# The last quarter of the columns of the masked product in pruning moved to GpSimd, its row sums to ScalarE

## The reference

```python
edge_scores = softmax(cos * H, axis=1)              # cos = xn @ xn.T
edge_mask = (edge_scores >= th_edge) & comp_mask[:, None]
H_pruned = H * edge_mask                            # the masked product
connectivity = H_pruned.sum(axis=1)                 # its row sums
node_scores = softmax(connectivity * feat_mag)
node_mask = (node_scores >= th_node) & (connectivity > 0)
vdeg = maximum(H_pruned.sum(axis=1), EPS)
edeg = maximum(H_pruned.sum(axis=0), EPS)           # its column sums
agg = (H_pruned.T * dv_isqrt) @ transformed * de_inv[:, None]
msg = dv_isqrt[:, None] * (H_pruned @ agg)
```

## Time and profile before

| what | us |
|---|---|
| median of 3 runs | 2627.26 (2624.27 to 2629.78) |
| the profiled execution | 2625.25 |
| its span, first to last instruction | 2623.5 |
| VectorE busy | 1647.2 (63%) |
| TensorE busy | 2146.1 (82%) |
| ScalarE busy | 768.6 (29%) |
| GpSimd busy | 4.1 |
| pruning's row blocks, first iteration | about 708 to 1068 |
| pruning's row blocks, second iteration | about 1691 to 2051 |

### The profile page before, as it was taken

One profiled execution on the slowest core, in us unless ns is written; L12 is line 12 of the kernel. 1 busy time (PEld: TensorE's weight loads), 2 busy tenths in 40 slices (PEclk: granted clock), 3 DMA queues, 4 the chain that ended last, 5 costly groups with the idle time before them and its releaser, 6 DMA issues. The chain is left out here.

```text
span 2623.5 us, 36440 instructions
## 1 busy us (share of the span) xinstructions
PE 2146.1 (82%) x15204; PEld 748.1 (29%) x15224; DVE 1647.2 (63%) x1785; ACT 768.6 (29%) x856; POOL 4.1 (0%) x16
## 2 busy tenths in 40 slices
PE   6769879799776566799999799776666799969998
PEld 2224243232221111244453233221111244432222
DVE  7870043288698888755523288698888755555553
ACT  0010010166443333111110166443333111125554
POOL 0000000000000000000000000000000000000000
PEclk9999989999887887899999999887887899979999
DMA  9958989799389898977779799389898977747770
GB/s 387 424 251 360 408 345 424 321 378 373 145 352 375 357 363 354 375 258 258 274 312 427 323 380 378 152 358 378 356 362 353 369 258 258 285 197 257 262 272 28
DMA packets 119369, 836.03 MB, mean 319 GB/s; under 512 B 8512, under 2 KB 10560, under 8 KB 76608
## 3 DMA queue, kind: packets, MB, share of 16 engines
q1 hardware_dynamic: 117184, 832.63, 80.4%
q10 hardware_dynamic: 2048, 1.35, 0.2%
HBM read 698.68 MB, written 135.27 MB: 318 GB/s over the span
## 5 line engine op out<-in xcount | busy, mean ns | idle before, releaser
L786 DVE CUSTOM_DVE_ANT_0 stream<-ps,stream 128x1024 f32<-128x1024 f32 x504 | 594.3, 1221 | 134.8 <-DMA stream<-in_adj 92.6
L797 ACT ACTIVATE stream<-stream,negmax 128x4096 f32<-128x4096 f32 x128 | 474.9, 3710 | 594.9 <-DVE negmax L791 594.9
L753 PE MATMUL ps<-edgeT,node_twice 64*128 64x512 f32 x1024 | 294.4, 699 | 253.1 <-DVE mx L786 253.1
L401 PE MATMUL ps<-stream,stage 128*64 128x512 f32 x1792 | 401.8, 599 | 62.1 <-DMA stream<-in_adjT 36.5
L1118 DVE SCALAR_TENSOR_TENSOR stream<-stream,cut 128x4096 f32<-128x4096 f32 x62 | 278.0, 4484 | 6.3
L753 PE MATMUL ps<-edgeT,query_twice 64*128 64x512 f32 x1024 | 245.4, 612 | 6.4 <-DVE edgeT L817 3.9
L1078 PE MATMUL ps<-stream,xw 32*64 32x512 f32 x4096 | 229.5, 589 | 0.6 <-ACT xw L1161 0.6
L753 PEld LDWEIGHTS ps<-edgeT,node_twice 64*128 64x128 f32 x1024 | 98.7, 210 | 440.6 <-DVE mx L786 330.4
L401 PEld LDWEIGHTS ps<-stream,stage 128*64 128x64 f32 x1792 | 127.0, 138 | 330.2 <-issue 285.1
L768 PE MATMUL ps<-stream,ones 128*1 128x512 f32 x1024 | 181.0, 844 | 8.2 <-DVE stream L1118 8.2
L1343 ACT ACTIVATE stream<-ps,bits_bias 128x1024 int32<-128x1024 f32 x128 | 142.4, 1114 | 108.1 <-PE ps L1308 107.2
(11 more groups left out here) (180 smaller groups left out, 1461.7 us busy)
## 6 DMA issues: line engine op xcount, KB each, us to landing
stream<-in_adj SPq DMA_DIRECT2D x178, 2048.0 KB, 11.8
stream<-in_adjT SPq DMA_DIRECT2D x74, 2048.0 KB, 12.2
pruned<-stream SPq DMA_DIRECT2D x64, 2048.0 KB, 7.7
spare<-pruned SPq DMA_DIRECT2D x22, 2048.0 KB, 11.2
query_twice<-pruned SPq DMA_DIRECT2D x22, 2048.0 KB, 11.4
node_twice<-pruned SPq DMA_DIRECT2D x20, 2048.0 KB, 11.5
query_twice<-in_adjT SPq DMA_DIRECT2D x7, 2048.0 KB, 35.3
node_twice<-in_adjT SPq DMA_DIRECT2D x7, 2048.0 KB, 35.2
```

The costliest lines, as they stand in the source:

```text
L401: last = nc.tensor.matmul(ps[F * h:F * h + F, bank + b, :], stage[:, t.k % SL, :], half_bank(src, b, h), start=False, stop=False, skip_gro ...
L753: last = nc.tensor.matmul(ps[:, 2 * slot + h, :], stationary[F * h:F * h + F, rows_n], bank_of(edgeT[F * h:F * h + F, :], c), start=True, ...
L786: nc.vector.tensor_tensor_reduce(out=prod[s][:, cols], in0=ps[:, 2 * slot:2 * slot + 2, :].rearrange("p a b -> p (a b)"), in1=block_in[:, ...
L797: nc.scalar.activation(prod[s], prod[s], ACT.Exp, bias=negmax[:, s:s + 1], accum_out=zsum[:, s:s + 1]).then_inc(exp_done, 1)
```

## The change

`prune(t)` on VectorE now does columns 0 to 3071 (`LEFT = 3 * CHUNK`) with the same instruction. GpSimd waits for `cut_ready` and does columns 3072 to 4095 in two instructions, a comparison with the cut in place, and, after a wait for its own first one, a product with the block in place. ScalarE copies these 1024 columns into an unused buffer for the sake of their row sums, one block later than its exponentials. SyncE's store and TensorE's column sums wait for both parts. VectorE waits for ScalarE's sums, before it takes the slot again and at the end, and adds the two row sums.

```diff
+                conn_right, conn_ready = st["mean"], sem("row_sums_added")
+                kept_right, right_summed = sem("right_columns_kept"), sem("right_columns_summed")
+                pruned, pruned_right = sem("left_columns_pruned"), sem("right_columns_pruned")
+                LEFT = 3 * CHUNK
+                unused = moved[:, 0:16, :].rearrange("p n f -> p (n f)")
...
                     def store(t):
                         s = t.k % SL3
                         sp.wait_ge(pruned, t.n + 1)
+                        sp.wait_ge(pruned_right, t.n + 1)
...
                         pe.wait_ge(pruned, t.n + 1)
+                        pe.wait_ge(pruned_right, t.n + 1)
...
                         nc.vector.scalar_tensor_tensor(
-                            out=prod[s], in0=prod[s], scalar=cut[:, s:s + 1], in1=buffer(t),
-                            op0=ALU.is_ge, op1=ALU.mult,
+                            out=prod[s][:, 0:LEFT], in0=prod[s][:, 0:LEFT], scalar=cut[:, s:s + 1],
+                            in1=buffer(t)[:, 0:LEFT], op0=ALU.is_ge, op1=ALU.mult,
                             accum_out=st["conn"][:, bass.ds(t.block, 1)]).then_inc(pruned, 1)
...
                         wait(dve, summed, t.n - 2)
+                        wait(dve, right_summed, t.n - 2)
...
                     dve.wait_ge(pruned, NB)
+                    dve.wait_ge(right_summed, NB)
+                    v = nc.vector
+                    v.tensor_tensor(st["conn"][:, :], st["conn"][:, :], conn_right[:, :], ALU.add)\
+                        .then_inc(conn_ready, 1)
+                    dve.wait_ge(conn_ready, 1)
+
+                @block.gpsimd
+                def _(pool):
+                    def body(t):
+                        s = t.k % SL3
+                        right = prod[s][:, LEFT:N]
+                        pool.wait_ge(cut_ready, t.n + 1)
+                        nc.gpsimd.tensor_scalar(right, right, cut[:, s:s + 1], None, ALU.is_ge).then_inc(kept_right, 1)
+                        pool.wait_ge(kept_right, t.n + 1)
+                        nc.gpsimd.tensor_tensor(right, right, buffer(t)[:, LEFT:N], ALU.mult)\
+                            .then_inc(pruned_right, 1)
+                    for n in range(NB):
+                        body(last_step(n, seq))
...
+                    def sum_right(t):
+                        act.wait_ge(pruned_right, t.n + 1)
+                        wait(act, right_summed, t.n)
+                        nc.scalar.activation(unused, prod[t.k % SL3][:, LEFT:N], ACT.Copy,
+                                             accum_out=conn_right[:, bass.ds(t.block, 1)]).then_inc(right_summed, 1)
+
+                    def body(t):
+                        exponentials(act, t, max_ready, exp_done)
+                        if t.k >= 1:
+                            sum_right(t.back(1))
+                    row_blocks(act, 3, LEAD, body, seq)
+                    sum_right(last_step(NB - 1, seq))
```

More of the change, by code:

```diff
@@ L927, in build @@
                 seen = sem("scores_seen")
-                exp_done, cut_ready, pruned = sem("exp_done"), sem("cut_ready"), sem("pruned")
+                exp_done, cut_ready = sem("exp_done"), sem("cut_ready")
+                conn_right, conn_ready = st["mean"], sem("row_sums_added")
[3 more added lines that the diff above has]
+                unused = moved[:, 0:16, :].rearrange("p n f -> p (n f)")
                 seq = [23, 24, 25, 26, 27, 28, 29, 30, 31, *range(23)]
@@ L1136, in _ @@
                     dve.wait_ge(pruned, NB)
+                    dve.wait_ge(right_summed, NB)
[15 more added lines that the diff above has]
+                        body(last_step(n, seq))
                 @block.scalar
                 def _(act):
-                    row_blocks(act, 3, LEAD, lambda t: exponentials(act, t, max_ready, exp_done), seq)
+                    def sum_right(t):
[9 more added lines that the diff above has]
+                    sum_right(last_step(NB - 1, seq))
                 @block.scalar
```

## The result

| | before | after |
|---|---|---|
| median of 4 runs each | 2627.56 (2624.27 to 2629.78) | 2728.22 (2726.75 to 2732.4) |
| ratio | | 1.0387, 95% interval 1.0369 to 1.0405 |
| the profiled execution / its span | 2625.25 / 2623.5 | 2728.66 / 2726.9 |

The change makes the kernel 101 us slower. 2702 was forecast, with 2740 as the upper end. The sign, the end and the reload came out near what was worked out, and the ring in its sum; a sixth of the loss stands where a small gain was forecast, at the start of the pass.

What follows compares the result with a forecast made beforehand. The two-step ring of load, scores, cut and pruning was taken to bound the kernel. Terms 29.3 - 1.1 + 6.3 + 3.9 = 38.4 us per iteration, 77 for both, on 2625.25 gave 2702 us; range 2612 to 2740.

Steps and rivals of the forecast that it cites:

- the end: Last but one cut to last pruned block: 15.5 us in place of 9.2, so +6.3 us per iteration.
- the reload: GpSimd reload between last product and first node reduction: 8.1 us, delaying the maximum by +3.9 us per iteration.
- the ring: The 24 load-bound steps of the pruning pass: 12.77 us each against 11.55, so +29.3 us per iteration.
- The bound: Pruning loop: a load waits for the block three back; half of R (cut until all columns pruned) counts per step.
- R = 7.8, in turns: Cut until all columns pruned: VectorE and GpSimd exclude each other, 7.8 us in place of 4.62; chance 0.60.
- The load term: Load's share of a two-step turn: 11.9 us, the median load of the kernel before, in a 25.5 us turn.
- The start: Blocks 0 to 4, before the first ring-bound load: four save 1.07 us, the fifth adds 3.2; -1.1 us per iteration.
- ScalarE and the column sums at no cost: Row blocks: ScalarE has room for its 1.3 us sums, TensorE reaches the later column sums during the next scores; no cost.
- Side by side: Rival: both engines prune concurrently, 4.2 us after the cut; 2612 us; chances faster 0.17, same 0.06, slower 0.04.
- Score passes that take turns with GpSimd: Rival: a 1.22 us score pass between GpSimd's comparison and product; 2734 us; within the 0.13 for slow or more exclusion.
- GpSimd slow, at R = 10.9: Rival: turns with slow GpSimd passes, all columns pruned 10.9 us after the cut; 2794 us; within a shared chance of 0.13.
- the load takes up slack: Rival: with longer steps every load lands in 11.6 us, a turn is 25.2; 2695 us, counted inside the main case.

Runs made afterwards that it cites:

- `written_out`: The changed kernel with VectorE's row-block loop written out in full, so no register instruction stands ahead of its product; 2756.83 us, ratio 1.0504.
- `strict_turns`: The changed kernel with GpSimd's comparison waiting for VectorE's left part in every block; 2771.21 us, ratio 1.0546.
- Experiment 6: The changed kernel with blocks 1, 2 and 3 stored with 16 of 128 rows, the other rows written ahead; 2714.46 us, ratio 1.0328.
- experiment 8: The kernel before, with a one-column GpSimd comparison behind the first and the last pruned block of each pass; 2632.11 us, ratio 1.0012.
- experiment 1: The kernel before, with GpSimd's comparison and product over 1024 columns of unused data at every cut, nothing in the row blocks waiting; 2648.46 us, ratio 1.0087.
- experiment 10: The changed kernel without ScalarE's sums over columns 3072 to 4095 and without the waits for them; 2725.13 us, ratio 1.0368.
- experiments 11 and 12: Spare block as fourth load buffer, loops written out: on the kernel before 2563.77 us, ratio 0.9751; on the changed kernel 2630.31 us, ratio 1.0011.

## Why the prediction was right, and where it was not

- **The bound** (half of R per step) is shown in the main: 0.48 from end to end over six kernels, with a load that differs by up to 0.7 us a turn between them, and 64 us gained where the ring is opened.
- **R = 7.8, in turns.** Its product of 2.35 is right to the hundredth. Its comparison, 1.65 from the 0.7 ns a column that an input adds in the earlier trace rows, is mis-sized: 2.84. With VectorE first the same working then gives the measured 8.6. The sentence that with the comparison first the end would be the same failed: VectorE loses 0.87 us to a comparison of 2.84, not all of it, and R is 6.6. In the mean over the ring steps it is 6.95.
- **The load term**, 11.9 as the median of the earlier trace rows, is mis-sized too. By the same working it is 12.9 (2 x 12.83 - 0.71 - 5.12 - 6.95), near the 12.65 of the kernel before. That loads would get shorter as the pairs of transfers lie further apart did not come out, at this R. The two errors cancel, 25.65 a turn against 25.53: the +29.3 is right by two wrongs of about 0.9 us a turn each. At R = 8.6 and above the load term does fall, to 12.3 in `written_out` and 12.5 in `strict_turns`, so that their steps grow by less than half of R.
- **The start failed: "Four of them save 1.07, the fifth lengthens R by 3.2".** It asked only when a load can leave, and not what else VectorE waits for. A block's slot is free when its store has landed. In the kernel before this costs next to nothing: the scores of block 6 begin 0.52 us late, at 764.77, with no releaser named, and the store of block 3, issued at 754.91, took 9.7 us to land, 0.2 us before. With R at 8.6 the stores leave later. Block 4 waits 4.01 us for one (timeline above), blocks 5 and 6 wait 3.01 and 1.76. The profile names no releaser for these two, but the stores in question, issued at 748.64 and 761.04, took 9.7 and 7.9 us to land, so they landed 0.5 and 0.2 us before the scores began, while the blocks' loads had landed over 5 us before. Only the waits of blocks 4 and 5, 7.0 us, lie ahead of the first load bound by the ring. With 4.3 saved, 4.1 for the longer R of the fifth block and some 1.0 of small waits they make the 7.8. Experiment 6 gives 6.1 us back by shorter stores alone. With the measured start in place of -1.1 the forecast would have been 2702 + 2 x 8.9 = 2720.
- **The end** (15.5, measured 15.2) is right in size by luck too. The first of the two blocks took 6.6, the second 8.6.
- **The reload** is right in kind, and near in size: 8.86 us ahead of the reduction in the first iteration, 8.30 in the second, with 8.1 predicted; alone it shows in experiment 8. That one row of 8.1 would fit so well was partly luck, since this gap was 6.1 to 10.6 us over the runs (10.63 in `strict_turns`). The Trainium skill, GPSIMD Engine Reference, Instruction dispatch, has about 6 us for such a load: the gaps of 6.05 and 6.97 us in experiments 1 and 8 lie near it, the 8.86 of the changed kernel does not.
- **ScalarE and the column sums at no cost** is right for ScalarE (experiment 10). The column sums of the last block do cost: at the granted clock of 0.50 they would hold the maximum's reader until 6.3 us behind the last product, were the reload not longer still.
- **Rivals.** Side by side fell with experiment 1: the data are not shared, and still the comparison takes 6.94. Score passes that take turns with GpSimd fell too: its product took 2.35 us beside score passes at 737.04 and 738.18. With GpSimd slow, at R = 10.9, fell: in after 8.6 is the most. That the load takes up slack appeared only at the highest R.

The Trainium skill, SBUF — State Buffer, section on the two separate sides, has the shared port pair held by one engine for a whole instruction. The traces agree wherever VectorE is first (3.94, 6.06 and 7.08 us), and for GpSimd's product, to whose end a VectorE instruction on one column is held (2.28 us, from 1102.41 to 1104.69). They disagree for a GpSimd comparison that is first: VectorE then gets through its 3072 columns with 0.87 us more.

## What to carry to other kernels

Before work is split between engines, name the circle that bounds the stage: here the wait ended with the later part, so relieving the busier engine could gain nothing, and a buffer more gained 64 us. Check every wait of the lengthened stretch, the stores of a slot as well as the loads, above all where a pass starts and the slack is another one than in its middle. Where a profile names no releaser, compare the landings of the transfers with the start that came late. In these runs VectorE and GpSimd held each other up even on data that they did not share: the split of one product between them was more a sequence than a pair, and GpSimd's time added to the path (R from 4.6 to 6.6 and 8.6).

## What the runs showed of the hardware

- GpSimd's comparison with a value per row takes 2.84 us over 128x1024 float32, longer than its product with two inputs, 2.35. The memsets and the masking instruction of the earlier trace rows were no measure of it.
- Which of two engines released by one semaphore starts first hung on 0.10 us more or less ahead of VectorE's product, and changed R by 2 us a block (6.6 and 8.6). It also hung on GpSimd's own start, 0.10 us behind the cut in the changed kernel and 0.17 in experiment 1.
- What the comparison takes from VectorE when it is first is 0.87 us for 1024 columns, whether VectorE has 1024 or 3072; a comparison over 512 columns takes 1.56 us and costs it 0.44 (4.39 in place of 3.95).
- The gap ahead of the first reduction after other GpSimd work was 6.1 to 10.6 us in these runs: 6.1 to 7.0 in experiments 1 and 8, 7.3 to 10.6 where GpSimd had pruned last. What sets it in this range is open.
- The loads of neighbouring steps come 9.7 and up to 17.4 us apart in the changed kernel. The short distance is VectorE's own work of a step (4.4 us from the cut to the end of its part, 5.2 from there to the next cut); the long one is the rest of the turn, with the wait for a load in it. Why one load takes 11.6 us to land and another 14.4 is open.
- The time of a store from issue to landing was 7.2 to 11.7 us in experiments 11 and 12 for the same 2 MB, the longest where the transfers were full.
